# Layer 0 attention: score products from six products of parts in two row tiles, scores made in one block per slot

## The reference

```
xn = layernorm(x)
q, v, k = split(xn @ Wqvk)                     # 16 heads of 8
scores[b,h,s,t] = q . k, masked t > s          # 256 x 256 per head
weights = softmax(scores / sqrt(128), over t)
x = x + (weights @ v) @ Wo + moe0(xn)          # top 2 of 8 experts, capacity 256
x = x + retention(layernorm(x)) ...; x = x + moe1(x)   # layer 1
```

## Time and profile before

| | us |
|---|---|
| median of 3 runs | 817.58 (817.22 to 819.66) |
| the profiled execution | 820.03 |
| its span, first to last instruction | 817.4 |
| TensorE busy | 741.1 (91%) |
| VectorE busy | 551.0 (67%) |
| ScalarE busy | 421.1 (52%) |
| GpSimd busy | 320.5 (39%) |
| first exponential of layer 0 starts | 66.1 |
| last one | 323.3 |
| mean granted TensorE clock | 0.967 |

### The profile page before, as it was taken

How to read it: one execution, slowest core, us unless ns; L and a number is a source line. 1 busy time by engine, 2 the same in 40 slices (tenths; PEclk the granted TensorE clock), 3 DMA queues, 4 the chain that set the end, 5 groups by cost and what they waited for, 6 DMA issues and landing times.

```text
span 817.4 us, 17712 instructions
## 1 busy us (share of the span) xinstructions
PE 741.1 (91%) x6148; PEld 579.7 (71%) x6148; DVE 551.0 (67%) x1059; ACT 421.1 (52%) x788; POOL 320.5 (39%) x408
## 2 busy tenths in 40 slices
PE   4767798998999998788988699999999999999997
PEld 3644566767776675676666588888888888888886
DVE  4955789764566776676987566666666666666665
ACT  4724545565556567866766344444444444444442
POOL 2752658462164876013777364121212121212111
PEclk9976989999999999997999799999999999999999
DMA  5773646242035551001211361112112111211100
GB/s 184 229 215 102 181 158 232 72 127 79 4 127 140 171 166 54 2 4 39 60 48 53 90 149 52 60 45 64 51 39 64 51 60 43 64 44 60 50 14 13
DMA packets 58131, 70.71 MB, mean 87 GB/s; under 512 B 6609, under 2 KB 37841, under 8 KB 58065
## 3 DMA queue, kind: packets, MB, share of 16 engines
q1 hardware_dynamic: 56320, 67.46, 27.5%
q0 software_dynamic: 1024, 2.10, 0.9%
q10 hardware_dynamic: 720, 0.27, 0.1%
HBM read 53.80 MB, written 15.86 MB: 85 GB/s over the span
## 4 chain that ended last, share of the span: by engine, by line
PE 74%; DVE 9%; issue 4%; DMA 4%; ACT 3%; POOL 2%; SPq 2%; ACTq 0%; DVEq 0%
PE ps L1660 23%; PE ps L1881 21%; PE ps L1769 3%; PE ps L1588 3%; PE ps L1571 3%; PE ps L1536 2%; DMA q_st<-m_neg 2%; PE ps L1519 2%; PE ps L1724 2%; PE ps L1568 1%; DVE m L1193 1%; PE ps L1689 1%; PE ps L1790 1%; PE ps L1532 1%; PE ps L1594 1%
## 5 line engine op out<-in xcount | busy, mean ns | idle before, releaser
L934 ACT ACTIVATE f_h<-ps 128x512 fp32r<-128x512 f32 x256 | 153.0, 598 | 197.3 <-PE ps L1660 197.3
L1407 DVE SCALAR_TENSOR_TENSOR f_l<-ps,f_h 128x512 fp32r<-128x512 f32 x256 | 175.9, 690 | 114.2 <-ACT f_h L934 113.0
L1660 PE MATMUL ps<-x_hl,w_h 128*128 (+1 forms) x512 | 201.3, 393 | 0.0
L766 POOL TENSOR_TENSOR acc<-acc,yt 128x512 f32<-128x512 f32 x55 | 70.9, 1290 | 249.8 <-DVE yt L1445 249.8
L850 ACT ACTIVATE probs<-ps 128x1536 f32<-128x1536 f32 x64 | 92.9, 1451 | 69.4 <-PE ps L1571 69.4
L1660 PEld LDWEIGHTS ps<-x_hl,w_h 128*128 128x128 f32 x512 | 96.7, 189 | 19.7
L1660 PE MATMUL ps<-x_hl,w_l 128*128 (+1 forms) x256 | 100.1, 391 | 0.0
L1881 PE MATMUL ps<-f_l,w_h 128*128 128x512 f32 x256 | 99.7, 390 | 0.4 <-DVE f_l L1407 0.4
L1881 PE MATMUL ps<-f_h,w_h 128*128 128x512 f32 x256 | 100.0, 391 | 0.0
L1881 PE MATMUL ps<-f_h,w_l 128*128 128x512 f32 x256 | 99.7, 389 | 0.0
L667 POOL TENSOR_SCALAR_AFFINE_SELECT probs<-probs 128x512 f32<-128x512 f32 x96 | 65.4, 705 | 77.3 <-ACT probs L850 77.2
(11 more groups left out here) (227 smaller groups left out, 1392.0 us busy)
## 6 DMA issues: line engine op xcount, KB each, us to landing
gate_b<-gate_rows SPq DMA_DIRECT2D x64, 256.0 KB, 3.2
k_st<-qk_parts SPq DMA_DIRECT2D x32, 288.0 KB
q_st<-qk_parts SPq DMA_DIRECT2D x96, 96.0 KB
qk_parts<-qk_p SPq DMA_DIRECT2D x16, 384.0 KB, 2.6
y_tok<-zero SPq DMA_DIRECT2D x8, 512.0 KB, 3.1
w_raw<-in_w_e SPq DMA_DIRECT2D x16, 256.0 KB, 2.9
x_rows<-xn_ring SPq DMA_DIRECT2D x16, 128.0 KB, 2.3
w_up<-in_w_up SPq DMA_DIRECT2D x8, 256.0 KB, 2.9
```

The costliest lines, as they stand in the source:

```text
L766: nc.gpsimd.tensor_tensor(acc[:, :], acc[:, :], yt[:, e % 2, :], ALU.add).then_inc(summed, 1)
L934: nc.scalar.activation(r32(f_h[:, m % 4, :]), ps[:, m % 4, :], ACT.Relu).then_inc(f_hi, 1)
L1407: nc.vector.scalar_tensor_tensor(out=r32(f_l[:, m % 4, :]), in0=ps[:, m % 4, :], scalar=0.0, in1=f_h[:, m % 4, :], op0=ALU.max, op1=ALU.su ...
L1660: last = nc.tensor.matmul(dst, r32(lhs[i]), r32(rhs[j]), start=(k == 0), stop=(k == 2))
```

## The change

Nine products of parts become six (those of middle by low, low by middle and low by low are dropped), so a stack has 48 rows and fits in half of the array's rows; two heads lie one above the other, at partitions 0 and 64, and their products go to two row tiles in turn. For this `keep_parts` stores nine slots per sequence instead of six, three of them copies of high parts that VectorE makes. The loads of a pair are four again, each of 48 rows, with 24 as the outermost count of the source. In each slot all scores of group n+3 and the turned scores of group n are made in one place, paired so that the two row tiles never write to one bank at once (two waits of TensorE on its own products guard that). `turn_out` and `divide` are done four slots behind instead of two, `weigh` two instead of one, `probs` has three buffers instead of two, the tail has six slots instead of four, `turn_heads` is split over two slots, and `index_out` over three.

```diff
-R0 = 9 * HD0
+R0 = 6 * HD0
+HALF = P // 2
+PARTS0 = 9
@@ SP
             def keep_parts(b, v):
+                sp.wait_ge(qk_twice, 2 * b + 2)
...
             def load_pair(b, half, r):
-                src = qk_rows[ds(b, 1), 1, :, half].rearrange("o r c -> (o r) c")
-                sp.dma_start(k_st[0:R0, r, :, :]..., src.unsqueeze(1).broadcast_to([rows, 3, 2 * GH * S]))
-                src = qk_rows[ds(b, 1), 0, :, half].rearrange("o (i d) c -> (o d) i c", d=HD0)
-                for j in range(3):
-                    sp.dma_start(q_st[j * rows:(j + 1) * rows, r, :, :]..., src)
+                for u in range(2):
+                    for st, slot, step in ((k_st, 0, 2), (q_st, 5, 1)):
+                        src = bass.AP(qk_parts.tensor, ((b * PARTS0 + slot) * P + (half * 2 + u) * GH) * S,
+                                      [[H0 * S, 3 * HD0], [step * P * S, 2], [1, GH * S]])
+                        sp.dma_start(st[u * HALF:u * HALF + R0, r, :, :]..., src)
@@ VectorE, first part
             def rest0(b, v):
...
+                nc.vector.tensor_copy(qk_p[:, v, 0:5:4, :], qk_p[:, v, 1:2, :].broadcast_to([P, 2, S])).then_inc(qk_twice, 1)
+                nc.vector.tensor_copy(qk_p[:, v, 7, :], qk_p[:, v, 5, :]).then_inc(qk_twice, 1)
@@ ScalarE, slot
-  put_heads0, exponential(g), negate_max(g+2), evacuate(g-1)
+  negate_max(g+2), evacuate(g-3), put_heads0, exponential(g)
@@ VectorE, slot
-  row_max_second(g+2), index_out, add_attention, divide(g-2), row_max_first(g+3), routing
+  row_max_late(g+2), row_max_early(g+2), divide(g-4), take_slots, add_attention, index_out, routing
@@ TensorE
+            def scores(g):
+                far = plus(g, 3)
...
+                for u in range(2):
+                    late(far, u, 0)
+                pe.wait_ge(exp_done, num(g))
+                pe.wait_ge(mrow_in[at(g, 4)], div(g, 4) * 16 + 16)
+                for n in range(2):
+                    left = early(far, 0, n)
+                    right = turned_second(g, 1, n)
+                left.then_inc(early_left, 1)
+                right.then_inc(st_right, 1)
+                for u in range(2):
+                    last = late(far, u, 1)
+                last.then_inc(late_done, 1)
+                for n in range(2):
+                    for u in range(2):
+                        turned_first(g, u, n)
+                pe.wait_ge(early_left, num(far) + 1)
+                pe.wait_ge(st_right, num(g) + 1)
+                for n in range(2):
+                    right = early(far, 1, n)
+                    left = turned_second(g, 0, n)
+                right.then_inc(early_done, 1)
+                left.then_inc(st_done, 1)
...
             def slot(g):
+                mask_late(plus(g, 3))        # waits late_max of n+2
+                attention_out(b) or turn_heads(b, t), where they are due
+                find_slots()                 # n == FIND
+                turn_out(plus(g, -4))
+                mask_t(g)                    # table slots; waits exp_done of n-1
+                turn_max(plus(g, 2))         # waits late_max and early_max of n+2
+                mask_early(plus(g, 3))       # waits early_max of n+2
+                scores(g)
+                weigh(plus(g, -2))
```

More of the change, by code:

```diff
@@ L131, in build @@
         tok = sb("tok", [P, 4, ST], where=era)
+        found = sb("found", [P, 5, ST], where=era)
         pick_p = sb("pick_p", [P, 2, NT], where=era)
@@ L1502, in _, with stacks @@
             pe.wait_ge(v_put, B + CREDIT)
[L1503 to L1505 removed]
+            pe.wait_ge(ones_row, 32)
+            def stacks(g, u, n, rows):
                 r = at(g, RING)
[L1508 to L1512 removed]
+                return (st[u * HALF:u * HALF + rows, r // 2, r % 2 * 2 + n, :] for st in (q_st, k_st))
@@ L1552, in scores_t @@
-            def scores_t(g):
-                r = at(g, RING)
-                qs, ks = (st[0:R0 + 1, r // 2, (r % 2) * GH:(r % 2) * GH + GH, :] for st in (q_st, k_st))
+                mask_late(g)
+                mask_early(g)
+                for n in range(2):
+                    for u in range(2):
+                        last = late(g, u, n)
+                last.then_inc(late_done, 1)
+                for n in range(2):
+                    last = early(g, 0, n)
+                last.then_inc(early_left, 1)
@@ L1624, in slot @@
-                if k == 3 and past(g, 7):
-                    attention_out(div(plus(g, -7), GPB0), u)
-                if within(g, G0):
-                    scores_t(g)
-                if num(g) == COUNT:
-                    pe.wait_ge(counted, 3)
-                if past(g, 2) and within(plus(g, -2), G0):
-                    turn_out(plus(g, -2))
-                if within(plus(g, 3), G0):
-                    scores_late(plus(g, 3))
+                    mask_late(plus(g, 3))
+                for b in range(B):
+                    if attention_added(b) == n:
+                        attention_out(b)
+                    for t in range(TB):
+                        if heads_turned(b, t) == n:
+                            turn_heads(b, t)
```

380 lines of the change are left out of this document (204 added, 176 removed).

## The result

Median of 12 runs 827.69 us (824.21 to 829.79) against 819.47 (815.66 to 824.66) for the kernel before in 12 runs on the same chip: ratio 1.0097, 95% interval 1.0074 to 1.012, so the changed kernel is about 1% slower. The forecast was 809.5, with a range of 800 to 821. The profiled execution has a span of 826.4 us against 817.4, 9.0 longer; the medians are 8.2 apart.

A forecast was written before the change was run, and what follows sets the result against it. TensorE was taken to bound plain and table slots, VectorE slots 9 to 19 and the first part; -5.0 - 4.9 + 0 + 2.4 - 1.5 + 0.9 = -8.1 from 817.58 gave 809.5 us, range 800 to 821.

The forecast's parts named there:

- Its own sign of being wrong for the slots of the routing: Interval from group 2 to group 20 changing by more than 2 us either way would show the forecast wrong.
- Score products in pairs: TensorE, each slot: two heads in two row tiles overlap, 1536 columns in 0.66 us instead of 3072 in 1.33.
- One block per slot: Last 24 plain slots: a ring of scores, maxima and VectorE's reductions takes 3.03 us against 3.24; -5.0 us.
- Table slots: Slots using the mask table: a ring through the exponential of 3.25, taken 3.3 against 3.63, over 15 intervals; -4.9 us.
- Row of maxima: Scores, layer 0: needed about 2 x 3.03 us after negation, so TensorE's stall goes; counted inside the 3.24.
- Slots 2 to 19: Layer 0 slots with mark_rows: VectorE's work is unchanged, so 0, bounds -2 and +2 us.
- find_slots: Its slot and the three after it, layer 0: the same, within 1 us.
- Tail: Last groups, weighed two and turned four slots later: one more round of turn, divide, turn; +0.9 us (0 to +2).
- First part: Sixteen sequences before the slots: two more VectorE copies each, 0.1 us over 12, 0.3 over the last four; +2.4 us.
- start: First stacks a third smaller, slots 0 to 2 at 1.2 GHz save TensorE work; -1.5 us (0 to -3).
- Rival 1: First part: second copy waits behind GpSimd's subtraction, some 0.95 us in each of 12 sequences; 819.7 us, chance 0.19.
- 2 (pairs not overlapping): Plain and table slots: row tiles take turns, rings grow to 3.35 and 3.95 us; 827 us, chance 0.08.

The follow-up runs named there:

- e6: Changed kernel with GpSimd's four instructions that place the choices at the end of its slot 5 instead of 6; ratio 1.0005 to the kernel before.
- e11: Kernel before with eight reductions that nothing reads added at the end of VectorE's slot 44; one run, 856.44 us.
- e12: Changed kernel with the same eight unread reductions added at the end of VectorE's slot 44; one run, 860.39 us.
- e2: Changed kernel with the 64 find_slots products and all that follows from them one slot later (21 instead of 20); ratio 0.9969 to the kernel before.
- e13: Changed kernel with the shorter tail alone (five slots instead of six, earlier copies, later square root); one run, 823.20 us (kernel before: median 819.84).
- e10: Changed kernel with 128 KB more written to DRAM per sequence of the first part; one run, 861.52 us (kernel before: one run, 850.84).
- e9: Kernel before itself, unchanged, as a profiled control on a slower chip; single run, groups 23 to 39 took 116.97 us.
- e5: Changed kernel itself, unchanged, as a control on a slower chip; 856.0 us, ratio 1.0033 to the kernel before.

## Why the prediction was wrong

From -8.1 to +9.0 is 17.1 us. Its own sign of being wrong for the slots of the routing was met by far: groups 2 to 20 took 83.38 us instead of 70.12, where 2 us either way were allowed. By its own steps:

- *Score products in pairs*: right by the trace. Records of the two row tiles start together (302.97; 303.09 and 303.10), and the block from 302.97 to the start of the weighing at 303.77 is 0.80 us for 1536 columns.
- *One block per slot, -5.0*: the mechanism was right, a ring with VectorE's reductions in it, TensorE idle ahead of what waits for them. It measured 2.89, not 3.03. The reductions take 1.82 (300.63 to 302.45), not 1.89, and the weight load of the maxima is not in series: 0.11 from their end to the transpose, not 0.05 + 0.11. Slots with attention work are not flat: 3.14 where TensorE's attention_out, 0.44 us and not 0.11 or 0.22, stands ahead of the turn of the maxima (275.06 to 275.50), and 3.21 where behind that VectorE's addition and statistics delay its reductions. Sum -8.1 instead of -5.0.
- *Table slots, -4.9*: the ring of 3.25 was 3.28 to 3.29 in five slots of seven, 3.6 in the others: -3.8, and +0.6 at the experts. Three quarters right.
- *Row of maxima*: right. TensorE waited for it once, 3.3 us, ahead of the first exponential; before 8 times, 6.5 us. The rule on engines that I cited there was put to no test.
- *Slots 2 to 19, 0 with bounds of 2*: **the first failed step**, +6.2 in groups 3 to 19. I argued from VectorE's sum of work, which was nearly right for groups 9 to 19 (+1.2). I did not ask when GpSimd's routing instructions would run. In slots 3 and 4 VectorE waits 2.31 us for one of them, and groups 2 to 5 lose 2.6 us; this is read from the trace, and no run tried it. In slots 7 and 8 it is the four that place the choices. Their input is there at 93.3 and they start at 99.77 (90.1 and 93.9 before): the exponential of group 6, behind whose cutting they stand, is now later after VectorE's scan, and the copy of values had moved from slot 5 into slot 6, ahead of them. VectorE is held 5.61 us instead of 2.35, and groups 7 to 9 lose 3.6. With the placing a slot earlier (e6) the hold was 2.37, and groups 5 to 11 took 27.21 us, the kernel before 27.17 to 27.34. e11 and e12 showed that a hold of one length costs both kernels alike, so what costs is that it grew.
- *find_slots "the same, within 1"*: **the second**, +4.5. The diff puts the products ahead of the block, where GpSimd's last tile is not ready: 2.35 us of waiting, and 1.95 more in the products, at a granted clock of 0.50. e2 removed both.
- *Tail, +0.9 (0 to 2)*: **the third**, +6.6. I priced one more round at 0.9. It was a chain of rounds over the one bank of weighed values (weigh, copy, turn, copy of heads, weigh), with the 1.28 us table load in it, and from 330 to 341 at a granted clock of 0.52. e13 took 2.6 to 3.1 off; the cause of the other 3.5 was not tested.
- *First part +2.4, start -1.5*: +3.7 and +1.6, less 2.1 in groups 0 to 3; together +3.4 with the 0.2 before them, instead of +0.9. The copies cost the forecast 0.1 a sequence where they are not held (2.43 against 2.32 to 2.40). Rival 1 came in part: six copies were held, not 12, and only two of them cost 0.8 us each (0.95 in my text), so that it explains some 1.6 of the 3.7. The row on which I had rested that rival, L1031, is no copy; the held copies of the changed kernel are its evidence. The stores, "just not the bound, but no cover is left", were the bound at the end: ScalarE waits for them, the first row of maxima is issued 5.7 us later than before, and with more to store (e10) the first exponential came at 75.96 instead of 71.57.
- *The clock* ran through all of it. The prediction counted it in the start alone, and else gave it one line ("may shift by one or two us"). Rows 5 had shown 0.50 in the stretch where the first slots wait. A wait of some us should have been priced with the slower work that follows it: e11 and e12 measure 1.6 to 2.0 us on top of 5.71.
- The chances for "slower" add up to 0.16 (0.08, 0.04 and 0.04) and not to 0.14.

The rivals: 2 (pairs not overlapping) gave 827, the measured time, by luck and for the wrong reason: the pairs overlap, and its place, plain and table slots, is where the change gained. Rival 1 had a true mechanism of too large a size. No rival held the one-off waits.

## What to carry over

Where a change reorders a software pipeline, its steady slots are the easy part: list the fixed events (one-off waits between engines, a prologue, a tail) and ask for each when its producer now runs and what was moved ahead of it in the producer's own order. Price a wait of TensorE together with the work that follows it at a lower granted clock. And when a stall seems to come from the new structure, put the same artificial hold into both kernels before believing it.

## What the runs showed of the hardware

- A hold of 5.71 us in VectorE cost 7.3 to 7.7 us in either kernel; the 64 products of find_slots took 2.46 to 2.47 us at a granted clock of 1.00 and 4.42 us at 0.50.
- In the changed kernel's profile VectorE's bf16 copy of 256 columns and GpSimd's instruction beside it start within 0.05 us of each other. Where the copy's recorded start is the earlier, it takes 0.22 us (30.30 before 30.35). Where it is 0.03 to 0.04 us the later, it takes 1.20 us in six sequences (50.89 after 50.86; the subtraction 1.16) and 0.22 in five (19.02 after 18.98; the subtraction 1.27). The Trainium skill (SBUF — State Buffer, "Who interferes with whom") says that of a VectorE copy in a fast mode and a GpSimd instruction whichever issues first has the shared ports for its whole length and the other is blocked. The lengths agree, one of the two being longer each time, but starts so close in the record do not tell which was first.
- Between the faster and the slower chips the kernel before differs by 31 to 35 us and the changed one by 28, nearly all of it in the stretch with indirect DMAs (31.3 of 33 us in e9, 26.7 of 29 in e5), and the ratio between the kernels with it (1.0097 and 1.0033).
